# r_pairs moved from the scores of group 2 to those of group 4, its values loaded late and unchecked, and the pieces around it laid anew

## The reference, cut to what matters

```python
x = x + L0_xattn(layernorm(x), ctx)      # 16 heads, softmax over 77 keys
x = x + L0_ffn(layernorm(x))             # relu FFN 256 -> 1024 -> 256, then layernorm
x = x + L1_xattn(layernorm(x), ctx)      # one head
idx = argmax(pe @ sign(tile_sigs).T, -1) # one of 8 matrices per position
x = x + (layernorm(x) @ W[idx].T + b[idx])
```

## Time and profile before

| | |
|---|---|
| runs | 271.34, 271.42, 272.66 us |
| profiled execution | 271.57 us, span 269.7 us |
| TensorE (PE) | 247.4 us busy, 92% |
| VectorE (DVE) | 218.2 us, 81% |
| GpSimd (POOL) | 189.6 us, 70% |
| ScalarE (ACT) | 160.7 us, 60% |
| chain that ended last | PE 70%, DVE 13%, POOL 5%, issue 4%, ACT 4%, DMA 2% |
| DMA | 17.61 MB, mean 65 GB/s |

### The profile page before, as it was taken

How to read it: one execution, slowest core, us unless ns; L and a number is a source line. 1 busy time by engine, 2 the same in 40 slices (tenths; PEclk the granted TensorE clock), 3 DMA queues, 4 the chain that set the end, 5 groups by cost and what they waited for, 6 DMA issues and landing times.

```text
span 269.7 us, 6211 instructions
## 1 busy us (share of the span) xinstructions
PE 247.4 (92%) x2048; PEld 219.3 (81%) x2048; DVE 218.2 (81%) x573; ACT 160.7 (60%) x510; POOL 189.6 (70%) x361
## 2 busy tenths in 40 slices
...
DMA packets 11156, 17.61 MB, mean 65 GB/s; under 512 B 1377, under 2 KB 7509, under 8 KB 11125
## 3 DMA queue, kind: packets, MB, share of 16 engines
...
...
## 4 chain that ended last, share of the span: by engine, by line
PE 70%; DVE 13%; POOL 5%; issue 4%; ACT 4%; DMA 2%; SPq 0%; POOLq 0%; DVEq 0%
PE PB L275 33%; PE PB L268 13%; PE PB L472 7%; PE PB L348 5%; PE S L396 5%; PE PB L408 4%; PE S L386 4%; ACT E L1067 2%; DVE SX L666 2%; DMA WKV<-in_w_k 2%; POOL E L1261 1%; DVE SX L680 1%; POOL SM L1218 1%; DVE XTL L645 1%; POOL out_x L1314 1%
## 5 line engine op out<-in xcount | busy, mean ns | idle before, releaser
L1261 POOL TENSOR_TENSOR E<-E,SX 128x308 f32<-128x308 f32 x64 | 43.9, 712 | 10.0 <-DVE SX L683 9.8
L1067 ACT ACTIVATE E<-S,SX 128x77 f32<-128x77 f32 x128 | 39.4, 337 | 10.7 <-DVE SX L666 10.7
L275 PE MATMUL PB<-XTH,W1H 128*128 128x256 f32 x128 | 37.3, 291 | 1.6 <-DVE XTL L645 1.4
L275 PE MATMUL PB<-W2H,HH 128*128 128x256 f32 x128 | 37.5, 293 | 0.0
L275 PE MATMUL PB<-W2H,HL 128*128 128x256 f32 x128 | 35.7, 279 | 0.0
L275 PE MATMUL PB<-W2L,HH 128*128 128x256 f32 x128 | 35.7, 279 | 0.0
L275 PE MATMUL PB<-XTL,W1H 128*128 128x256 f32 x128 | 35.6, 278 | 0.0
L275 PE MATMUL PB<-XTH,W1L 128*128 128x256 f32 x128 | 35.5, 278 | 0.0
L1218 POOL TENSOR_TENSOR SM<-SM,nhalf 128x2 f32<-128x2 f32 x40 | 28.4, 711 | 3.1
L1090 ACT ACTIVATE HH<-PB 128x512 fp32r<-128x512 f32 x32 | 19.1, 600 | 15.9 <-PE PB L275 15.6
L1077 ACT ACTIVATE EW<-S 124x640 f32<-124x640 f32 x32 | 21.9, 711 | 10.8 <-PE S L396 10.7
...
## 6 DMA issues: line engine op xcount, KB each, us to landing
...
```

The costliest lines, as they stand in the source:

```text
L275: t = e.matmul(dst, a, b, start=first and j == 0, stop=last and j == n - 1)
L1067: t = e.activation(Ei[:, h * NK:(h + 1) * NK], P[:, at:at + NK], ACT.Exp, bias=SX[:, i, 0, k:k + 1], accum_out=SX[:, i, 1, k:k + 1])
L1261: t = e.tensor_tensor(Eh, Eh, SX[:, i, 2, 8 * a + h:8 * a + h + 4].unsqueeze(2).to_broadcast([128, 4, NK]), ALU.mult)
```

## The change

Three things change. The first is one argument of the helper that loads EV into registers:

```diff
-            values = nc.values_load_multi_w_load_instructions(EV[0:1, row, 0:NP], engines=[e.engine],
-                                                              min_val=0, max_val=most)[1]
+            values = nc.values_load_multi_w_load_instructions(
+                EV[0:1, row, 0:NP], engines=[e.engine], min_val=0, max_val=most,
+                skip_runtime_bounds_check_because="each is a count of seven comparisons times a constant")[1]
```

```diff
...
-            hl(0, 3); apply("B", 1); lo("A", 3); r_pairs(); lo("B", 1); ssum(2, 1, 1); ql(3); y(0); stats("A", 4)
...
+            smax(5, 0, 0); lo("B", 3); apply("A", 6); ssum(4, 1, 0); cm(0); ssum(4, 1, 1); r_pairs(); ssum(5, 0, 0)
...
```

More of the change, by code:

```diff
@@ L535, in tensor @@
[L535 to L544, removed]
@@ L964, in vector @@
             smax(0, 0, 1); f_stats(); lo("A", 1); ssum(0, 0, 0); smax(0, 1, 0); smax(0, 1, 1); ssum(0, 0, 1); vb(0)
-            ssum(0, 1, 0); r_ranks(); ql(1); r_expert(); ssum(0, 1, 1); smax(1, 0, 0); lo("A", 2); smax(1, 0, 1)
-            stats("A", 3); ssum(1, 0, 0); ssum(1, 0, 1); f_norm(); smax(1, 1, 0); ql(2); smax(1, 1, 1); x1(0)
-            ssum(1, 1, 0); stats("B", 0); r_position(); smax(2, 0, 0); ssum(1, 1, 1); apply("B", 0); smax(2, 0, 1)
-            f_kv(0); f_kv(1); vb(1); lo("B", 0); ssum(2, 0, 0); smax(2, 1, 0); smax(2, 1, 1); kbl(1); r_index()
@@ L969, in vector @@
-            ssum(2, 0, 1); apply("A", 3); hl(0, 0); hl(0, 1); x1(1); ssum(2, 1, 0); stats("B", 1); hl(0, 2); f_m()
-            hl(0, 3); apply("B", 1); lo("A", 3); r_pairs(); lo("B", 1); ssum(2, 1, 1); ql(3); y(0); stats("A", 4)
-            smax(3, 0, 0); smax(3, 0, 1); hl(1, 0); apply("A", 4); stats("Y", 0); f_q(); hl(1, 1); x2(0); ssum(3, 0, 0)
-            ssum(3, 0, 1); hl(1, 2); hl(1, 3); f_c(); stats("C", 0); smax(3, 1, 0); smax(3, 1, 1); lo("A", 4)
-            stats("A", 5); stats("A", 6); y(1); apply("A", 5); x1(2); ssum(3, 1, 0); ssum(3, 1, 1); stats("B", 2); f_o()
@@ L989, in vector @@
[L989 to L992 removed]
+            ssum(0, 1, 0); r_ranks(); ql(1); ssum(0, 1, 1); stats("A", 3); lo("A", 2); f_norm(); smax(1, 0, 0)
@@ new lines, in vector @@
+            smax(1, 0, 1); r_expert(); vb(1); ssum(1, 0, 0); smax(1, 1, 0); ql(2); smax(1, 1, 1); ssum(1, 0, 1)
+            ssum(1, 1, 0); x1(0); ssum(1, 1, 1); stats("B", 0); smax(2, 0, 0); r_position(); apply("B", 0)
+            smax(2, 0, 1); apply("A", 3); f_kv(0); ssum(2, 0, 0); lo("B", 0); f_kv(1); smax(2, 1, 0); ssum(2, 0, 1)
+            lo("A", 3); r_index(); x1(1); stats("B", 1); smax(2, 1, 1); apply("B", 1); hl(0, 0); ssum(2, 1, 0); f_m()
+            ql(3); hl(0, 1); ssum(2, 1, 1); hl(0, 2); hl(0, 3); smax(3, 0, 0); kbl(1); smax(3, 0, 1); f_q()
@@ new lines, in vector @@
+            ql(5); apply("B", 3); stats("C", 1); ssum(4, 0, 1); hl(2, 1); hl(2, 2); hl(2, 3); apply("C", 1)
+            smax(5, 0, 0); lo("B", 3); apply("A", 6); ssum(4, 1, 0); cm(0); ssum(4, 1, 1); r_pairs(); ssum(5, 0, 0)
+            hl(3, 0); hl(3, 1); y(2); smax(5, 0, 1); hl(3, 2); stats("Y", 2); smax(5, 1, 0); x2(2); x3_(0); x1(4)
+            stats("C", 2); hl(3, 3); ssum(5, 0, 1); lo("A", 6); smax(5, 1, 1); apply("C", 2); cm(1); stats("B", 4)
+            apply("A", 7); ssum(5, 1, 0); ssum(5, 1, 1); y(3); stats("Y", 3); ql(6); cm(2); lo("A", 7); apply("B", 4)
```

152 lines of the change are left out of this document (80 added, 72 removed).

## The result

The changed kernel takes 276.22 us (median of four, 275.18 to 276.96) where the kernel before takes 271.95 in the same set (271.34 to 272.66): ratio 1.0155, 95% interval 1.0119 to 1.0191. The forecast was 268.2. The profiled execution, the fastest of the four, is 275.18 us with a span of 273.3, 3.61 more than that of before.

What follows compares the result with a forecast made beforehand. It took TensorE as the bound from 50.24 to 229.85 us, VectorE as setting the pace in the front. Sum: 271.57 + 0.3 - 2.7 + 0.6 - 1.5 = 268.3, less 0.15 for the median: 268.2, range 265.8 to 270.9.

Steps and rivals of the forecast that it cites:

- Bias gathers and weight loads: 0: GpSimd's gathers and SyncE's weight loads, issued later: no cost, since their results are first read late, by bd(0) and pr(0).
- I allow 2 us of waits ... lo(B,1) ends at 71.7: VectorE's way to lo(B,1): 18.6 us plus 2 for ScalarE's hh and hi, ending 1.3 us before it is needed.
- The gain that rested on it: TensorE from tE(1,1,1) to w1(1,0): 2.7 us won by itself, 2.4 with the 0.3 lost ahead taken off.
- 0.3 late: TensorE up to tE(1,1,1): 0.3 us lost, waiting in both orders for the subtraction of smax(2,0,1), ending near 50.5.
- a fall only behind 50 us: Sign of being wrong: a TensorE clock below 1.00 behind 50 us, which no row of before shows there.
- r_pairs: 0.6 taken: r_pairs between ssum(4,1,1) and ssum(5,0,0) on VectorE: 0.6 us lost, with 0.5 to spare before hl(3,0) is needed.
- Rival 1: r_pairs stalls TensorE by 1.8 to 4.5 us more before pv(4,0) or sc(5,1,1): 270.1 to 272.8; chance 0.13.
- The unchecked loads 0: Loads without check instructions, behind lo(B,6) on VectorE and ahead of ex(7,0,0) on ScalarE: 0 us, covered by TensorE's work.
- the tail 1.5: Tail behind w2(7): 1.5 us won of 2.65 lost, by moved pieces that fill TensorE's waits around tC(7).
- Rival 2: Slower: r_pairs is stretched at its new place on VectorE by GpSimd beside it, doubled throughout giving 275; chance 0.07.

Runs made afterwards that it cites:

- e5: Changed kernel with GpSimd's bo(7) and be(6) moved away from gathers, gx(5) moved behind b2(0), and VectorE's stats(A,5) moved behind x2(0): 270.69 us, ratio 0.9955.
- e9: e5 with the lists of the kernel before up to pv(1): 270.58 us, ratio 0.9935.
- e6: Kernel before with r_pairs moved behind ssum(4,1,1), its loads unchecked and late, and bs(0) behind en(5,0,1): 281.63 us, ratio 1.0358.
- e2: Changed kernel with two GpSimd pieces moved, bo(7) to behind bs(4) and be(6) to behind rs(C,5): 273.51 us, ratio 1.0060.
- e1: Changed kernel with the lists of the kernel before up to pv(1,1), smax(2,1,0), hi(B,0) and en(2,0,0): 274.82 us, ratio 1.0126.
- e8: e6 with r_pairs one piece later on VectorE, behind apply(C,1): 274.75 us, ratio 1.0087.
- e4: Kernel before with only the 30 checks left out of the three loads of EV: 271.67 us, ratio 1.0012.
- e3: Kernel before up to w2(7), hl(7,3), hh(7,3) and bd(2), then the changed order of the tail: 270.16 us, ratio 0.9950.
- e11: e9 up to w2(4), then the order of the kernel before up to w2(7), then the changed tail: 272.21 us, ratio 1.0023.

## Why the prediction was wrong

**The step that failed is one that the sum didn't have.** "Bias gathers and weight loads: 0" counted who reads their results and found it late; that holds. But GpSimd's list was otherwise treated as cover only, and what a piece of it does to its neighbours wasn't priced: six gathers in a row, two additions behind a gather and the stats(A,5) that reads the gathered tokens cost 5.5 us (e5) of the 8.0 between 268.2 and 276.22. The diff showed both changes, since GpSimd's order was among those laid anew.

**"I allow 2 us of waits ... lo(B,1) ends at 71.7": it ended at 75.67.** The allowance named hh and hi, not ssum(3,0,0), which stands just ahead of lo(B,1) in the order rows and needs ex(3,0,0), behind hi(B,1) on ScalarE. With the gathers spread it ends at 74.78 (e5), still 3.1 later than that. TensorE, late itself, didn't wait for it at w1(1,0); the wait came out at tE(2,1,1), behind y(0). The gain that rested on it was right in its cause: with GpSimd mended, 1.51 us at w1(1,2) (e9), 1.6 with r_pairs alone (e6), where 2.4 were forecast. In the changed kernel it came too (2.34 between 52.61 and 80.52) and was used up to make good the late tE(1,1,1).

**"0.3 late" at tE(1,1,1): 2.37.** The prediction took it that tE(1,1,1) waits for the subtraction of smax(2,0,1) in both orders. In the changed one it has the bank of sc(2,0,0), not of sc(2,0,1), and it starts at 52.61 without idle time, 0.05 us after the subtraction began (VectorE's timeline):

```profile
52.56 0.80 DVE L672 TENSOR_TENSOR E<-S,SX 128x616 f32<-128x616 f32 x1
```

The loss stands ahead of it: two waits of 1.05 and 0.89 and, behind them, a clock of 0.51 from 48 to 50 us; the prediction had named a fall only behind 50 us, as a mark of being wrong. Without the fall the same order is 0.82 (e2) and 0.96 late (e5). With tE(1,1,1) 3.1 us earlier (e1) 1.4 came back by medians, with GpSimd mended 0.1 (e5 to e9): the loss is mostly covered by the next wait.

**r_pairs: 0.6 taken, 0.4 measured up to sc(5,0,1), without a wait of TensorE.** The count of what TensorE still had to do, against what queues on VectorE, held; no run put r_pairs back to its old place in the changed order, so this rests on the trace. Rival 1's waits at pv(4,0) and sc(5,1) came only in before's order (e8), where e6 also shows one wait of 6.60: the step was right for the list as it was written, and says nothing of r_pairs as such.

**The unchecked loads 0, the tail 1.5:** right (271.67 against 271.61 in e4; 1.45 in e3, 1.40 in the changed kernel). The covers held: at the old place TensorE was never late for y(2) (e4), at the new one VectorE's cm(4), behind the loads, waits 2.81 us for TensorE's cs(4) and starts at 202.34.

**The rivals.** Rival 2 gave 275 for the case that VectorE is held beside GpSimd, at 0.07. Held VectorE instructions were half of the loss, but the place was wrong: it isn't r_pairs, which took 6.14 us instead of 7.37, but two pairs of x2. That the time came out near is chance. For the other half no rival stood. The Trainium skill's "SBUF — State Buffer", section "SBUF: two separate sides", says that one instruction holds the shared ports wholly and the other engine blocks meanwhile. By that rule x2 would have waited for one addition at most (1.42 / 2 = 0.71 us); the trace differs in length: it began beside the gather, and its end came when both additions were done.

**Even mended the kernel reaches 270.58, not 268.2.** The middle loses 2.1 us from w1(1,2) to w2(7) (-1.51 to +0.61 in the table) where 0.6 were taken. By stage in e9, columns as in the earlier trace rows, from behind wo(3) to the end of w2(7):

```profile
103.83:230.46 126.63, 125.37 (x1099) 115.46 (x1098) 107.05 (x279) 78.49 (x255) 89.66 (x171) 1.00 0.20 58
```

That is 1.26 us idle, 0.40 and 0.39 of it in two waits, at tB(6) and tB(7), that the trace puts down to "issue"; before has 0.13 in nearly the same stretch. (This execution is 1.1 above the median, but 0.9 of that lies behind the start of pr(14), 8.9 us to the end instead of 8.0.) e11 tried to take it back and failed, so what causes it stays open. In e9 the front wins 1.51, the middle loses 2.12 and the tail wins 1.39: with GpSimd mended, the whole change is worth no more than its tail alone, which e3 has.
